# A hybrid block on one core: a new order of the stage between samples, and six of 32 scan inputs made by GpSimd

## The chip, the cores and the metric

One core of a Trainium2 chip runs the whole program. The metric is the device time of one execution in microseconds (us), the median of several runs. Engines: PE is TensorE, DVE is VectorE, ACT is ScalarE, POOL is GpSimd, SP is SyncE, which here only issues DMAs.

## The reference, cut to what matters

For each of 8 samples (800 tokens of 128 channels) three layers follow one another:

```
x = x + mamba(groupnorm(x))        # state space layer; its output gets the residual groupnorm(x) too
t = t + attention(layernorm(t))    # 8 heads of 16, softmax, projection, relu
t = t + experts(layernorm(t))      # two experts per sample, after all samples
```

The inner part of the mamba layer, with 256 inner channels and 16 states:

```
xz = xr @ W_in.T;  xc, z = split(xz)
xc = silu(causal_conv4(xc) + conv_b)
dt_in, Bm, Cm = split(xc @ W_xproj.T)
dt = softplus(dt_in @ W_dt.T + b_dt)
dA = exp(dt * A);  dBu = (dt * xc) * Bm        # u = dt * xc, times B
h = dA_t * h + dBu_t;  y = sum_states(h * C_t) # the scan over 32 time steps
out = ((y + xc * D) * silu(z)) @ W_out.T;  out = out * rsqrt(mean(out^2)) * ln_w
```

## The kernel before, in words

Every engine has its own list of instructions, written out by hand in one Python function per engine, and semaphores (`sig`) tie them together. All work is float32 except the bfloat16 parts of the attention scores.

Time is cut in turns. `turns` (line 481 on) calls `steps(n, m, f)` and then `front(n, m, f)` for each turn, where m is the sample whose scan runs, n = m - 1 the sample in attention, and f = m + 1 the sample that is prepared. Turn 0 has no n, turn 7 no f, and turn 8 only n.

**Steps.** The scan of one sample is 32 steps (`NSTEP`). A step i covers 32 channels times 4 states on 128 partitions and 800 columns. On each engine it is:
- DVE: the product of u and b, `PS<-u_rep,b_rep` (L1237, called P(i) below), into PSUM bank 2, then the scan `hst<-dA,PS` (L1242, S(i)), which reads dA from SBUF and the product from PSUM.
- ACT: `dA<-dt_rep,a_sb` (L924, the decay), up to three steps ahead, since dA has three buffers.
- POOL: `...<-hst,c_rep` (L794, G(i)), the multiplication by C. It waits for S(i) and also for P(i+1), in the code `pool.wait_ge(dbu_ready.sem, dbu_ready.at(m, i + 2))`.
- PE: once per four steps, `sum_states` (L1389).

hst has two buffers, so S(i) waits for G(i-2):

```
if i >= 2:
    dve.wait_ge(g_ready.sem, g_ready.at(m, i - 1))
```

**Attention among the steps.** In steps `MAX_FROM` = 5 to `MAX_TO` = 7 the row maxima of the scores are found: 50 items, each of PE products (L1508, L1509, L1514), a ReLU on ACT (L965) and a DVE reduction (L1263). The items need `k_neg`, made by DVE (L1258) from `k_stack`, which comes by DMA. From `UNIT_FROM` = 9 to `UNIT_TO` = 30 come 100 units: PE scores (L1542), ACT exponential (L975), PE product with V (L1527), and per 25 units one DVE copy to o_raw (L1284).

**Front.** Between S(31) and the next sample's S(0), each engine finishes attention of n and the mamba output of m, and prepares f. The chains of DVE in the order of the code: divide the attention (L1135, L1140); convolve chunk 0 (L1101, L1104); sum_up and gate of m (L1080, L1151); convolve chunk 1; attention residual t2 and the sums of its norm, norm2 (L1158, L1020 to L1030); the RMS factor of m (`rms_v` L1164, then POOL's reciprocal root L727, then L1168); relu of dt (L1173); residual of m (L1177); softplus rest, dt and u of f (L1117 to L1128); the sums of norm1 (L1020 to L1030); `x_sum` of f (L1187); statistics of the next sample's group norm (L1044 to L1063). ACT in the front: silu of both chunks (L850), squares of m's output (L873), xd (L877), |dt| (L858), exp and ln (L898, L902), silu of z (L854), then norm1 applied (L840) and the decay of the next step 0 (L924). norm1 is applied with POOL's result of L727 and L737, which wait for the sums on DVE (`ln1_var`).

Of the kernel before, what the change touches and what calls it, by code (L numbers as in the profile page):

```python
# [32 lines left out]
def mamba_attention_moe(nc, x, w_in_t, conv_w, conv_b, w_xp_t, w_dt_t, b_dt, a_log, d_skip, w_out_t,  # L33
# [46 lines left out]
    with ctx:  # L80
# [239 lines left out]
        dbu_ready = sig("dbu_ready", NSTEP)  # L320
# [23 lines left out]
        parts_out = sig("parts_out", 32)  # L344
# [479 lines left out]
        def _(act):  # L824
# [19 lines left out]
            def front(n, m, f):  # L844
# [30 lines left out]
                if f is not None:  # L875
                    act.wait_ge(xd_up.sem, xd_up.at(f, 1))
                    nc.scalar.copy(xd[:, :], wide(2)).then_inc(xd_ready.sem, 1)  # L877
                    absolute(0)
                    exp_of(f, 0)
                    ln_of(f, 0)  # L880
# [4 lines left out]
                    nc.scalar.activation(dt_sb[:, 1, :], wide(0), ACT.Relu, bias=b_dt_sb[:, 1:2]).then_inc(dt_relu1.sem, 1)  # L885
                if m is None and f is not None:
# [796 lines left out]
```

## Time and profile before

| | before |
|---|---|
| median of 3 runs | 1777.21 us (1776.51 to 1780.95) |
| the profiled execution | 1784.96 us, span of its instructions 1783.4 us |
| DVE busy | 1381.3 us, 77% |
| PE busy | 1210.5 us, 68% |
| ACT busy | 1089.9 us, 61% |
| POOL busy | 702.1 us, 39% |
| mean granted TensorE clock | 0.823 |

How to read it: the time is that of the engine or chain that ends last in each stage, and the stages repeat with the turns. A busy share below 100% on every engine means that the bound moves between engines, or that one waits for another; which of them must be read stage by stage from the timeline of a turn.

### The profile page before, as it was taken

Reading aid. Unit: us, or ns where it says so; the run is one execution under the profiler, and the core shown is the slowest. Engines: PE = TensorE matmul, PEld = TensorE weight load, DVE = VectorE, ACT = ScalarE, POOL = GpSimd, SP = SyncE. Lnnn points to the kernel's source line nnn. Section 1 sums busy time; section 2 is a strip of 40 time slices with the busy share of each in tenths; the row PEclk is TensorE's granted clock in tenths of the full one; section 3 lists DMA queues with packets and bytes.
Section 4 is the critical chain, followed back from the end, with each engine's and each line's share of the span. In section 5 each row is a group of like instructions: output and inputs, shape, how many; then the busy total and the mean of one; then the engine's idle time right before and its main releaser. Section 6 shows DMA issues by size and latency. Waiting matters only on the chain. (4 is left out here: it accounts for less than half of the span.)

```text
span 1783.4 us, 21758 instructions
## 1 busy us (share of the span) xinstructions
PE 1210.5 (68%) x7072; PEld 520.4 (29%) x7072; DVE 1381.3 (77%) x2336; ACT 1089.9 (61%) x1993; POOL 702.1 (39%) x399
## 2 busy tenths in 40 slices
PE   5124577867786678667876787578847864884991
PEld 2002231242224222422233223222323222222871
DVE  4798788988898889888988988798879973401575
ACT  3432767676767677667757776677677844663430
POOL 3364235524561356225622553256324640000354
PEclk8555688978898789878996899689968996895996
DMA  2441634145414641363228231814072405003541
GB/s 68 158 138 28 187 56 158 38 168 102 149 47 141 129 146 41 122 158 123 64 69 210 74 113 42 228 57 138 23 193 84 139 10 111 2 1 94 164 128 51
DMA packets 94021, 185.08 MB, mean 104 GB/s; under 512 B 15512, under 2 KB 48564, under 8 KB 93908
## 3 DMA queue, kind: packets, MB, share of 16 engines
q1 hardware_dynamic: 92500, 180.41, 35.0%
q0 software_dynamic: 1408, 3.29, 0.6%
q8 instruction: 55, 0.90, 0.2%
q14 instruction: 58, 0.48, 0.1%
HBM read 146.47 MB, written 36.86 MB: 103 GB/s over the span
## 5 line engine op out<-in xcount | busy, mean ns | idle before, releaser
L1242 DVE TENSOR_TENSOR_SCAN hst<-dA,PS 128x800 f32<-128x800 f32 x256 | 466.2, 1821 | 36.8 <-ACT dA L924 3.6
L975 ACT ACTIVATE probs<-PS 128x400 f32<-128x400 f32 x800 | 343.6, 526 | 119.5 <-PE PS L1542 119.4
L1542 PE MATMUL PS<-q_stack,k_stack 99*128 99x400 bf16 (+1 forms) x896 | 238.4, 358 | 88.7 <-ACT probs L975 41.7
L924 ACT ACTIVATE dA<-dt_rep,a_sb 128x775 f32<-128x775 f32 x256 | 245.6, 962 | 74.4 <-DVE hst L1242 62.9
L1237 DVE TENSOR_TENSOR PS<-u_rep,b_rep 128x800 f32<-128x800 f32 x256 | 267.5, 1045 | 19.0 <-DMA u_rep<-u_dram 6.5
L965 ACT ACTIVATE probs<-PS 128x400 f32<-128x400 f32 x400 | 201.7, 504 | 120.1 <-PE PS L1509 97.5
L1263 DVE CUSTOM_DVE_ANT_0 probs<-PS,probs 128x400 f32<-128x400 f32 x400 | 219.7, 573 | 42.6 <-PE PS L1514 17.2
L1527 PE MATMUL PS<-probs,v_ext 128*32 128x400 f32 (+1 forms) x1792 | 206.1, 538 | 30.7 <-DVE o_raw L1284 24.1
L1508 PE MATMUL PS<-k_stack,q_stack 96*128 96x400 bf16 (+1 forms) x448 | 142.4, 354 | 96.7 <-DVE k_neg L1258 96.7
L794 POOL TENSOR_TENSOR dt_sb<-hst,c_rep 128x800 f32<-128x800 f32 x72 | 135.8, 1886 | 153.5 <-DVE PS L1237 153.5
L727 POOL TENSOR_TENSOR norm_r<-norm_r,neg_half 100x8 f32<-100x8 f32 x24 | 40.8, 1702 | 390.6 <-DVE norm_r L1030 371.9
L794 POOL TENSOR_TENSOR sp_l<-hst,c_rep 128x800 f32<-128x800 f32 x72 | 135.5, 1882 | 117.3 <-DVE PS L1237 117.0
L1542 PEld LDWEIGHTS PS<-q_stack,k_stack 99*128 99x128 bf16 (+1 forms) x896 | 66.8, 98 | 337.9 <-ACT probs L975 229.4
L1514 PE MATMUL PS<-k_stack,q_stack 96*128 96x400 bf16 (+1 forms) x448 | 142.0, 353 | 9.7 <-DVE q_max L1263 9.1
L1389 PE MATMUL PS<-dt_sb,fold 128*32 128x512 f32 (+1 forms) x288 | 109.6, 625 | 50.9 <-POOL lnT L794 36.6
L1509 PE MATMUL PS<-k_neg,q_stack 96*128 96x400 bf16 (+1 forms) x448 | 141.8, 352 | 0.0
L794 POOL TENSOR_TENSOR conv_acc<-hst,c_rep 128x800 f32<-128x800 f32 x32 | 60.1, 1878 | 182.6 <-DVE PS L1237 182.6
L1389 PE MATMUL PS<-sp_l,fold 128*32 128x512 f32 (+1 forms) x288 | 109.6, 626 | 0.0
L794 POOL TENSOR_TENSOR xd<-hst,c_rep 128x800 f32<-128x800 f32 x40 | 75.2, 1881 | 64.7 <-DVE PS L1237 64.7
L794 POOL TENSOR_TENSOR lnT<-hst,c_rep 128x800 f32<-128x800 f32 x40 | 76.1, 1902 | 37.3 <-DVE PS L1237 34.0
L1389 PE MATMUL PS<-xd,fold 128*32 128x512 f32 (+1 forms) x160 | 67.6, 549 | 19.7 <-POOL sp_l L794 10.6
L1284 DVE COPY o_raw<-PS 128x400 f32<-128x400 f32 x32 | 18.2, 567 | 77.9 <-PE PS L1527 77.9
(223 smaller groups left out, 2093.8 us busy)
## 6 DMA issues: line engine op xcount, KB each, us to landing
b_rep<-b_dram SPq DMA_DIRECT2D x64, 400.0 KB, 3.5
c_rep<-c_dram SPq DMA_DIRECT2D x64, 400.0 KB, 3.8
dt_rep<-dt_dram SPq DMA_DIRECT2D x64, 400.0 KB, 6.3
u_rep<-u_dram SPq DMA_DIRECT2D x64, 400.0 KB, 6.3
q_stack<-parts_dram SPq DMA_DIRECT2D x96, 100.0 KB, 4.7
k_stack<-parts_dram SPq DMA_DIRECT2D x96, 100.0 KB, 6.2
dt_dram<-dt_sb SPq DMA_DIRECT2D x16, 400.0 KB, 3.5
u_dram<-sp_l SPq DMA_DIRECT2D x16, 400.0 KB, 3.8
```

What stands on the lines that cost most here:

```text
L794: nc.gpsimd.tensor_tensor(g(i), hst[:, i % 2, :], c_rep[:, rnd % NBB, :], ALU.mult).then_inc(g_ready.sem, 1)
L924: nc.scalar.activation(dA[:, i % NDA, :].rearrange("p (j t) -> p j t", t=T)[:, :, 1:T], dt_rep[:, gi, :].rearrange("p (j t) -> p j t", t=T ...
L965: nc.scalar.activation(probs[:, k % NPROB, :], bank(5 + 2 * (k % 2), HALF), ACT.Relu).then_inc(relu_ready.sem, 1)
L975: nc.scalar.activation(probs[:, j % NPROB, :], bank(4 + j % 3, HALF), ACT.Exp, scale=ATT_SCALE).then_inc(probs_ready.sem, 1)
L1237: nc.vector.tensor_tensor(dbu, u_rep[:, gi, :], b_rep[:, k, :], ALU.mult).then_inc(dbu_ready.sem, 1)
L1242: nc.vector.tensor_tensor_scan(hst[:, i % 2, :], dA[:, i % NDA, :], dbu, 0.0, ALU.mult, ALU.add).then_inc(scan_done.sem, 1)
L1263: nc.vector.tensor_tensor_reduce(probs[:, j % NPROB, :], bank(4 + 2 * (j % 2), HALF), probs[:, j % NPROB, :], 1.0, LOWEST, ALU.add, ALU.ma ...
L1389: last = nc.tensor.matmul(PS[gi * DG:(gi + 1) * DG, at:at + width], fold[:, :], g(rnd * NG + gi)[:, at:at + width], start=(sg == 0), stop= ...
L1508: nc.tensor.matmul(bank(5 + 2 * (k % 2), HALF)[strip], q, k_stack[0:KST, h, HALF:TOK], start=True, stop=False)
L1514: last = nc.tensor.matmul(bank(4 + 2 * (j % 2), HALF)[strip], q, k_stack[0:KST, h, 0:HALF], start=True, stop=True)
L1527: last = nc.tensor.matmul(PS[32 * q:32 * (q + 1), 7 * BANK:7 * BANK + HALF], v_ext[keys, kt, h, :], probs[keys, j % NPROB, :], start=(kt = ...
L1542: last = nc.tensor.matmul(bank(4 + j % 3, HALF)[strip], k_stack[:, h, kt * P:kt * P + strip.stop - strip.start], q_stack[:, h, q0:q0 + HAL ...
```

## The change: what it does

1. **Products by POOL.** In steps 10, 14, 18, 22, 26 and 30 (`POOL_STEPS`) DVE makes no product. POOL makes it (`product`, L791 in the new code) right behind G(i-3), into `sp_e[:, 0, :]` in SBUF, and the scan of such a step reads both operands from SBUF. Semaphores count both kinds of product apart (`by_vector`, `by_pool`).
2. **Row maxima later.** `MAX_FROM, MAX_TO` go from 5, 7 to 7, 9, so the 100 units start at step 11 instead of 9 and still end before step 30. The first `k_neg` is made ahead of step 7's product, and the stacks of q load when q's own parts have been stored.
3. **Front.** On DVE both convolutions stand in a row; relu, softplus rest, dt and u of f go ahead of the RMS work of m; `x_sum` leaves DVE (PE adds x with a second product into PSUM, ACT copies it out after `ln1_var`); `group_var` goes behind S(0) and `group_apply` behind S(1). On ACT xd, |dt|, exp and ln go ahead of the squares. On PE the chunk products move and out_project is cut in halves.

The diff, cut to its core:

```diff
+        dbu_pool = sp_e[:, 0, :]
...
-        MAX_FROM, MAX_TO = 5, 7
+        MAX_FROM, MAX_TO = 7, 9
+        POOL_STEPS = [i for i in range(MAX_TO, NSTEP) if i % NG == 2]
...
             def load_u(m, ck, gi):
                 if ck > 0:
-                    sp.wait_ge(dbu_ready.sem, dbu_ready.at(m, ck * NSG * NG - NG + gi + 1))
+                    sp.wait_ge(dbu_ready.sem, dbu_ready.at(m, by_vector(ck * NSG * NG - NG + gi + 1)))
+                    sp.wait_ge(dbu_pool_ready.sem, dbu_pool_ready.at(m, by_pool(ck * NSG * NG - NG + gi + 1)))
...
+            def product(m, i):
+                ck, sg, gi, rnd = step(i)
+                pool.wait_ge(u_in[gi].sem, u_in[gi].at(m, 16 * (ck + 1)))
+                pool.wait_ge(b_in[rnd % NBB].sem, b_in[rnd % NBB].at(m, 16 * (rnd // NBB + 1)))
+                nc.gpsimd.tensor_tensor(dbu_pool, u_rep[:, gi, :], b_rep[:, rnd % NBB, :], ALU.mult).then_inc(dbu_pool_ready.sem, 1)
...
                         if i + 1 < NSTEP:
-                            pool.wait_ge(dbu_ready.sem, dbu_ready.at(m, i + 2))
+                            pool.wait_ge(dbu_ready.sem, dbu_ready.at(m, by_vector(i + 2)))
                         nc.gpsimd.tensor_tensor(g(i), hst[:, i % 2, :], c_rep[:, rnd % NBB, :],
                                                 ALU.mult).then_inc(g_ready.sem, 1)
                         if n is not None and i == MAX_FROM:
                             softplus_of_second_chunk(m)
+                        if i + 3 in POOL_STEPS:
+                            product(m, i + 3)
...
                 if f is not None:
                     silu_x(1)
+                    act.wait_ge(xd_up.sem, xd_up.at(f, 1))
+                    nc.scalar.copy(xd[:, :], wide(2)).then_inc(xd_ready.sem, 1)
+                    absolute(0)
+                    exp_of(f, 0)
+                    ln_of(f, 0)
                 if m is not None:
                     act.wait_ge(out_up.sem, out_up.at(m, 1))
                     for k in range(NT):
                         last = nc.scalar.activation(sq[:, k, :], tokens(4)[:, k, :], ACT.Square, accum_out=rms_v[:, 0, k:k + 1])
                     last.then_inc(rms_sq.sem, 1)
                 if f is not None:
-                    act.wait_ge(xd_up.sem, xd_up.at(f, 1))
-                    nc.scalar.copy(xd[:, :], wide(2)).then_inc(xd_ready.sem, 1)
-                    absolute(0)
-                    exp_of(f, 0)
-                    ln_of(f, 0)
                     silu_z(0)
                     silu_z(1)
...
+                    act.wait_ge(gn_tok_up.sem, gn_tok_up.at(f, 1))
+                    if m is not None:
+                        act.wait_ge(ln1_var.sem, ln1_var.at(m, 1))
+                    nc.scalar.copy(x_sum[:, :, :], tokens(6)).then_inc(xs_ready.sem, 1)
...
                     convolve(0)
+                    convolve(1)
...
+                if f is not None:
+                    dve.wait_ge(dt_abs.sem, dt_abs.at(f, 1))
+                    nc.vector.tensor_scalar(dt_sb[:, 0, :], wide(2), b_dt_sb[:, 0:1], 0.0, ALU.add, ALU.max).then_inc(dt_relu0.sem, 1)
+                    low_part(0, fthen)
+                    dt_and_u(0)
                 if m is not None:
                     dve.wait_ge(rms_sq.sem, rms_sq.at(m, 1))
...
-                    nc.vector.tensor_tensor(x_sum[:, :, :], x_tok[:, :, :], tokens(6), ALU.add).then_inc(xs_ready.sem, 1)
...
                 for i in range(NSTEP):
+                    if n is not None and i == MAX_FROM:
+                        negate_keys(0)
...
-                        nc.vector.tensor_tensor(dbu, u_rep[:, gi, :], b_rep[:, k, :], ALU.mult).then_inc(dbu_ready.sem, 1)
+                        source = dbu_pool if i in POOL_STEPS else dbu
+                        if i not in POOL_STEPS:
+                            nc.vector.tensor_tensor(dbu, u_rep[:, gi, :], b_rep[:, k, :], ALU.mult).then_inc(dbu_ready.sem, 1)
...
-                        nc.vector.tensor_tensor_scan(hst[:, i % 2, :], dA[:, i % NDA, :], dbu, 0.0,
+                        nc.vector.tensor_tensor_scan(hst[:, i % 2, :], dA[:, i % NDA, :], source, 0.0,
                                                      ALU.mult, ALU.add).then_inc(scan_done.sem, 1)
...
                     if f is not None and i == 0:
+                        group_var(f)
+                    if f is not None and i == 1:
                         group_apply(f)
```

Two places where instructions move. The first is POOL's list in a turn's steps, around steps 11 to 18 (`...<-hst,c_rep` is G of one step, by the buffer it writes; `sp_e<-u_rep,b_rep` is the new product). Before, from G(10) on:

```order
L794 TENSOR_TENSOR conv_acc<-hst,c_rep 128x800 x2
L794 TENSOR_TENSOR dt_sb<-hst,c_rep 128x800
L794 TENSOR_TENSOR sp_l<-hst,c_rep 128x800
L794 TENSOR_TENSOR xd<-hst,c_rep 128x800
L794 TENSOR_TENSOR lnT<-hst,c_rep 128x800
```

In the changed kernel, from G(10) on:

```order
L813 TENSOR_TENSOR conv_acc<-hst,c_rep 128x800 x2
L791 TENSOR_TENSOR sp_e<-u_rep,b_rep 128x800
L813 TENSOR_TENSOR dt_sb<-hst,c_rep 128x800
L813 TENSOR_TENSOR sp_l<-hst,c_rep 128x800
L813 TENSOR_TENSOR xd<-hst,c_rep 128x800
L813 TENSOR_TENSOR lnT<-hst,c_rep 128x800
L791 TENSOR_TENSOR sp_e<-u_rep,b_rep 128x800
```

A product stands between G(11) and G(12), and the next one behind G(15), so POOL has five operations per four steps where it had four.

The second is DVE's list in the front, behind the last small operation of norm2. Before:

```order
L1030 TENSOR_TENSOR norm_r<-norm_mv 100x8
L1164 TENSOR_SCALAR rms_v<-rms_v 100x8
L1168 SCALAR_TENSOR_TENSOR hst<-PS,rms_v,ln_w_sb 100x128 x8
L1173 TENSOR_SCALAR dt_sb<-PS,b_dt_sb 128x800
L1177 TENSOR_TENSOR t<-x_sum,hst 100x1024
L1117 TENSOR_SCALAR lnT<-sp_e 128x800
L1118 TENSOR_TENSOR lnT<-sp_e,lnT 128x800
L1121 TENSOR_TENSOR dt_sb<-dt_sb,lnT 128x800
L1126 TENSOR_TENSOR dt_sb<-dt_sb,sp_l 128x800
L1128 TENSOR_TENSOR sp_l<-dt_sb,xc 128x800
L1020 BN_STATS norm_stats<-t 100x6 x8
```

In the changed kernel:

```order
L1055 TENSOR_TENSOR norm_r<-norm_mv 100x8
L1187 TENSOR_SCALAR dt_sb<-PS,b_dt_sb 128x800
L1142 TENSOR_SCALAR lnT<-sp_e 128x800
L1143 TENSOR_TENSOR lnT<-sp_e,lnT 128x800
L1146 TENSOR_TENSOR dt_sb<-dt_sb,lnT 128x800
L1151 TENSOR_TENSOR dt_sb<-dt_sb,sp_l 128x800
L1153 TENSOR_TENSOR sp_l<-dt_sb,xc 128x800
L1193 TENSOR_SCALAR rms_v<-rms_v 100x8
L1197 SCALAR_TENSOR_TENSOR hst<-PS,rms_v,ln_w_sb 100x128 x8
L1203 TENSOR_TENSOR t<-x_sum,hst 100x1024
L1045 BN_STATS norm_stats<-t 100x6 x8
```

The work of sample f (relu, softplus rest, dt, u) now stands ahead of the RMS work of m, and the sums of norm1 come straight behind that.

## Rows read from the trace of the kernel before

**Rows 1.** Windows of turn 2: length, busy PE, PEld, DVE, ACT, POOL, clock, DMA
```profile
409.34:450.64 41.30, 33.51 (x191) 14.06 (x191) 33.26 (x112) 27.30 (x53) 12.36 (x7) 0.91 0.38 81
450.64:529.49 78.85, 63.59 (x434) 16.23 (x435) 71.79 (x54) 60.78 (x124) 48.02 (x25) 0.89 0.31 106
529.49:570.62 41.13, 28.56 (x144) 17.81 (x142) 33.79 (x77) 25.61 (x43) 10.35 (x8) 0.87 0.30 102
```

**Rows 2.** Timeline, steps 28 and 29 of turn 2: start, length, engine, line, operation, [idle before]
```profile
520.17 1.82 DVE L1242 TENSOR_TENSOR_SCAN hst<-dA,PS 128x800 f32<-128x800 f32 x1
...
522.02 1.00 DVE L1237 TENSOR_TENSOR PS<-u_rep,b_rep 128x800 f32<-128x800 f32 x1
...
523.15 1.82 DVE L1242 TENSOR_TENSOR_SCAN hst<-dA,PS 128x800 f32<-128x800 f32 x1
...
520.21 1.92 POOL L794 TENSOR_TENSOR lnT<-hst,c_rep 128x800 f32<-128x800 f32 x1 [1.18 <-DVE PS L1237]
```

**Rows 3.** Timeline, steps 21 to 23 of turn 2, and L1242 over the whole run
```profile
498.43 1.00 DVE L1237 TENSOR_TENSOR PS<-u_rep,b_rep 128x800 f32<-128x800 f32 x1
498.44 2.74 POOL L800 TENSOR_TENSOR conv_acc<-xc,z_act 128x800 f32<-128x800 f32 x1
...
501.14 1.92 POOL L794 TENSOR_TENSOR lnT<-hst,c_rep 128x800 f32<-128x800 f32 x1
501.42 2.49 DVE L1237 TENSOR_TENSOR PS<-u_rep,b_rep 128x800 f32<-128x800 f32 x1
...
L1242 DVE TENSOR_TENSOR_SCAN hst<-dA,PS x256: 1819/1821/1823, 63.3 to 1448.4; 128x800 f32<-128x800 f32 x128
```

**Rows 4.** Timeline, DVE, start of the maxima in turn 2
```profile
411.37 0.57 DVE L1258 TENSOR_SCALAR k_neg<-k_stack 96x1600 bf16<-96x1600 bf16 x1 [2.03 <-DMA k_stack<-parts_dram]
...
414.09 0.57 DVE L1263 CUSTOM_DVE_ANT_0 probs<-PS,probs 128x400 f32<-128x400 f32 x1 [2.15 <-PE PS L1514]
```

**Rows 5.** Timeline, turn 2: first and last exponentials of the units; first o_raw copy
```profile
455.81 1.69 ACT L975 ACTIVATE probs<-PS 128x400 f32<-128x400 f32 x4 [2.37 <-PE PS L1542]
...
524.00 2.07 ACT L975 ACTIVATE probs<-PS 128x400 f32<-128x400 f32 x5
...
475.56 0.57 DVE L1284 COPY o_raw<-PS 128x400 f32<-128x400 f32 x1 [2.04 <-PE PS L1527]
```

**Rows 6.** Timeline, DVE, second half of the front of turn 2
```profile
548.01 0.17 DVE L1164 TENSOR_SCALAR rms_v<-rms_v 100x8 f32<-100x8 f32 x1
...
551.68 2.16 DVE L1168 SCALAR_TENSOR_TENSOR hst<-PS,rms_v,ln_w_sb 100x128 f32<-100x128 f32 x8 [3.50 <-POOL rms_v L727]
...
554.71 1.22 DVE L1177 TENSOR_TENSOR t<-x_sum,hst 100x1024 f32<-100x1024 f32 x1
...
559.65 0.99 DVE L1128 TENSOR_TENSOR sp_l<-dt_sb,xc 128x800 f32<-128x800 f32 x1
...
562.96 0.17 DVE L1030 TENSOR_TENSOR norm_r<-norm_mv 100x8 f32<-100x8 f32 x1
563.04 1.22 DVE L1187 TENSOR_TENSOR x_sum<-x_tok,PS 100x1024 f32<-100x1024 f32 x1
...
570.62 1.82 DVE L1242 TENSOR_TENSOR_SCAN hst<-dA,PS 128x800 f32<-128x800 f32 x1 [0.55 <-ACT dA L924]
```

**Rows 7.** Timeline, ACT and POOL in the same stretch
```profile
545.79 0.30 ACT L873 ACTIVATE hst<-PS 100x128 f32<-100x128 f32 x1
...
550.00 1.64 POOL L727 TENSOR_TENSOR rms_v<-rms_v,neg_half 100x8 f32<-100x8 f32 x1
550.97 0.93 ACT L858 ACTIVATE sp_e<-PS,b_dt_sb 128x800 f32<-128x800 f32 x1 [1.70 <-PE PS L1377]
...
555.39 0.87 ACT L902 ACTIVATE sp_l<-sp_e 128x800 f32<-128x800 f32 x1
...
565.15 3.18 ACT L840 ACTIVATE probs<-t,norm_r 100x128 f32<-100x128 f32 x8 [1.51 <-POOL norm_r L737]
...
569.65 0.94 ACT L924 ACTIVATE dA<-dt_rep,a_sb 128x775 f32<-128x775 f32 x1
```

More of the change, by code:

```diff
@@ L343, in mamba_attention_moe @@
         v_copied = sig("v_copied")
-        parts_out = sig("parts_out", 32)
+        parts_out = [sig(f"parts_out{i}", 16) for i in range(2)]
         NSTK = 2 * len(Q_PARTS)
@@ L432, in share, with by_vector, by_pool @@
             return range(min(lo * work // (end - first), work), min(hi * work // (end - first), work))
+        def by_vector(k):
+            return sum(i not in POOL_STEPS for i in range(k))
+        def by_pool(k):
+            return sum(i in POOL_STEPS for i in range(k))
         def max_share(i):
@@ L866, in front @@
                     act.wait_ge(proj_up.sem, proj_up.at(n, 1))
-                    nc.scalar.activation(oT[:, :], wide(6), ACT.Relu, bias=proj_b_sb[:, 0:1]).then_inc(att_ready.sem, 1)
+                    nc.scalar.activation(oT[:, :], wide(4), ACT.Relu, bias=proj_b_sb[:, 0:1]).then_inc(att_ready.sem, 1)
                 if f is not None:
                     silu_x(1)
+                    act.wait_ge(xd_up.sem, xd_up.at(f, 1))
[3 more added lines that the diff above has]
+                    ln_of(f, 0)
                 if m is not None:
@@ L1152, in front @@
                                             ALU.mult).then_inc(y_ready[1].sem, 1)
-                if f is not None:
-                    convolve(1)
                 if n is not None:
@@ L1203, in front @@
                     group_mean(f + 1)
-                    group_var(f + 1)
                 assert n is None or dve_order_p.count == dve_order_p.per_turn, dve_order_p.count
@@ L1222, in low_parts, with negate_keys @@
                     dve.wait_ge(qk_parts.sem, qk_parts.at(n, i + 1))
+                def negate_keys(half):
+                    dve.wait_ge(stacks_in[half].sem, stacks_in[half].at(n, 16 * NSTK))
+                    nc.vector.tensor_scalar(k_neg[:, 4 * half:4 * half + 4, :], k_stack[0:KST, 4 * half:4 * half + 4, 0:HALF],
+                                            -1.0, None, ALU.mult).then_inc(k_neg_ready.sem, 1)
                 for i in range(NSTEP):
+                    if n is not None and i == MAX_FROM:
+                        negate_keys(0)
                     if m is not None:
@@ L1454, in front @@
                     last.then_inc(attT_up.sem, 1)
+                if f is not None:
+                    pe.wait_ge(silu_done.sem, silu_done.at(f, 2))
+                    x_project(1).then_inc(xd_up.sem, 1)
                 if m is not None:
@@ L1458, in front @@
                         pe.wait_ge(y_ready[ck].sem, y_ready[ck].at(m, 1))
-                    out_project(range(NT)).then_inc(out_up.sem, 1)
+                    out_project(range(NT // 2))
                 if f is not None:
-                    for ck in range(NC_):
-                        pe.wait_ge(silu_done.sem, silu_done.at(f, ck + 1))
-                        last = x_project(ck)
-                    last.then_inc(xd_up.sem, 1)
                     pe.wait_ge(xd_ready.sem, xd_ready.at(f, 1))
                     over_spans(2, w_dt_sb[DT0:P, 0:P], xd[DT0:P, :]).then_inc(dt_up.sem, 1)
+                if m is not None:
+                    out_project(range(NT // 2, NT)).then_inc(out_up.sem, 1)
+                if f is not None:
+                    if m is not None:
+                        pe.wait_ge(y_summed.sem, y_summed.at(m, NC_))
                     project_in(0, 2).then_inc(xz_up.sem, 1)
@@ L1470, in front @@
                         pe.wait_ge(t2_ready.sem, t2_ready.at(n, 1))
+                    pe.wait_ge(x_in.sem, x_in.at(f, 16))
                     for k in range(NT):
-                        last = nc.tensor.transpose(PS[0:TT, 6 * BANK + k * C:6 * BANK + (k + 1) * C], xnT[:, k * TT:(k + 1) * TT], ident[:, :])
+                        o = PS[0:TT, 6 * BANK + k * C:6 * BANK + (k + 1) * C]
+                        nc.tensor.matmul(o, xnT[:, k * TT:(k + 1) * TT], ident[:, :], start=True, stop=False)
+                        last = nc.tensor.matmul(o, ident[0:TT, 0:TT], x_tok[:, k, :], start=False, stop=True)
                     last.then_inc(gn_tok_up.sem, 1)
```

53 lines of the change are left out of this document (25 added, 28 removed).

## The prediction, made before the changed kernel was run

> **What bounds the kernel now.** I read the stages of a turn first, then the timeline inside each, then who ended the waits. Turn 2 stands for turns 1 to 6. The stretch of the row maxima lasts 41.30 us, steps 7 to 31 last 78.85, from the start of S(31) to the next S(0) pass 41.13 [rows 1]. VectorE has the highest busy share in the last two, 71.79 of 78.85 and 33.79 of 41.13; in the maxima TensorE and VectorE share it.
>
> In a step VectorE alternates: a scan of 1.82 us, a product of 1.00, and gaps, together 2.98 from scan to scan (520.17 to 523.15); I use 3.0 [rows 2]. GpSimd starts G within 0.04 us of the next scan, takes 1.92, and is then idle until the next product is done (1.18 idle). So GpSimd looks as if it had over a third of its time free, and that is what the change spends. The next two things to see decide whether it has.
>
> First, the two engines exclude each other in some operations. At 501.14 GpSimd began a G (both operands in SBUF), and 0.28 us later VectorE began a product, again with both operands in SBUF. It took 2.49 instead of 1.00, and ended 0.85 us after G [rows 3]. The other way round, at 498.43 and 498.44, VectorE's product came first and took its 1.00, and GpSimd's operation took 2.74. A scan, which has only dA in SBUF and the product in PSUM, ran beside a G in nearly every step and never took more than 1823 ns [rows 3]. The Trainium skill states this as a rule (SBUF — State Buffer, Who interferes with whom): a VectorE instruction with two SBUF inputs and a GpSimd one that reads SBUF exclude each other for the whole instruction, the later one being blocked. By that rule a scan that reads its product from SBUF is exposed as well, which no row here shows.
>
> Second, hst has two buffers, so S(i) waits for G(i-2). Today G(i-2) ends at about the end of S(i-1), and the product hides the rest.
>
> **The change part by part.**
>
> *Products by GpSimd.* Count from the start of S(i-2), where i is a step whose product GpSimd makes. G(i-3) runs 0.04 to 1.92. P(i-1) runs 1.85 to 2.85, and the new product, issued behind G(i-3), finds VectorE ahead of it, as at 498.44: it ends at about 4.65 (1.92 + 2.74) [rows 3]. S(i-1) runs 3.0 to 4.8. G(i-2) is queued behind the new product: 4.65 to 6.55. S(i) waits for it, until 6.6, where VectorE alone would have been ready at 4.9. In that instant GpSimd has already begun G(i-1), whose waits are met. If the scan with two SBUF operands is excluded like the product at 501.42, it starts at 8.4 and ends at 10.2; P(i+1) and S(i+1) follow, S(i+1) starting at 11.4. Before, this distance was three steps, 9.0. The price is 2.3 us per such step (rounding 2.4 down for gaps that overlap). The bounds: if GpSimd's work costs nothing, the step is worth -1.1 (the 3.0 of a step less 1.82 and a gap); if scan and G go side by side, S(i) runs 6.6 to 8.4 and S(i+1) starts at 9.5, +0.5; if the new product gets ahead of P(i-1), +2.6. I take 2.3, since the nearest row for two SBUF operands against a G is the 2.49, in full.
>
> In step 10 the new product is made during the maxima and costs nothing, and only the exclusion of S(10) by G(9) is left: 1.8 of waiting less the 1.1 saved, 0.7. So turn 0, which has no attention, pays 6 x 2.3 = 13.8, and turns 1 to 7 each pay 5 x 2.3 + 0.7 = 12.2.
>
> *Maxima two steps later.* VectorE's work is the same, only in another order. What goes is the wait of k_neg for the stacks, 2.03, since steps 5 and 6 (6.0 us) now stand ahead, and the wait for the first score, 2.15, since k_neg is made a step before it is needed [rows 4]. -4.2 per turn. In the units the first o_raw copy waits 2.04 for TensorE [rows 5]; the price of step 14 lies ahead of that copy and takes its place: -2.0.
>
> *Do the units now become the bound?* They ran from 455.81 to 526.07, 70.3 us [rows 5], with two decays of 0.94 in it that now lie ahead: 68.4. With the same distances to the scans they need some 71 from S(11) to S(31). VectorE: 78.85 - 6.0 - 2.0 + 12.2 = 83 from S(9), 76 from S(11) [rows 1]. So they stay hidden while VectorE pays its price, and would be the floor if it did not.
>
> Per turn 1 to 7: 12.2 - 4.2 - 2.0 = +6.0, x 7 = +42.
>
> *The front.* Today VectorE finishes norm2's sums at 548.0, waits 3.50 for GpSimd, and does the RMS work while ACT makes exp and ln [rows 6, 7]. In the new order it waits at the same place for |dt|, 550.97 + 0.93 = 551.9; that time hardly moves, because silu of chunk 1 still waits for the gate of m, which now stands behind both convolutions, and the half of out_project that is gone from TensorE's queue ahead of chunk 1's projection is replaced by the other half ahead of dt. Relu ends at 552.9, the softplus rest starts with exp at about 554, and dt and u end at 558.7, 1.9 us earlier than the 560.6 of today. But u is not what S(0) waits for: it waits 0.55 for ACT's decay at 569.65, which stands behind norm1's application, 565.15 to 568.33 [rows 6, 7]. And that chain starts later: squares (2.2 us, 545.79 to 548.0) now follow ln, which ends 556.26, so they are done at 558.5; then rms_v 0.17 at 558.7, GpSimd's root 1.64 and hand-over to 560.7, 2.16 for L1168, 1.22 for the residual, 2.5 for the sums (560.64 to 563.13): 566.6 instead of 563.13. From there to S(0) it is 7.5 us as today; ACT's copy of x_sum lies beside GpSimd's root. S(0) starts at 574.1 instead of 570.62: +3.4. The 1.22 of x_sum that VectorE no longer does lay beside that chain and brings nothing. group_var, two small operations of 0.16 and 0.15, is now behind S(0): +0.35. Together 3.75, in 7 fronts: +26. Bounds for a front: -1.6 (x_sum and group_var off the path, no later chain) and +5, if TensorE at its lower clock makes more of it late.
>
> On SP's queue the q stacks go out earlier and the loads of u wait for GpSimd's products too, which are done steps ahead: 0.
>
> **The sum.** 42 + 13.8 + 26 = +82 us on the profiled execution's 1784.96, 1867. The median of the runs is 7.7 lower, so 1859.
>
> **The rivals.**
>
> *A: scan and G do not exclude each other.* A scan is not the product of the row, and only the exclusion of products is seen. Then the price is 0.5, VectorE would need 67 from S(11), and the 71 of the units are the floor: 6.0 - 5 - 0.7 = about 0 per turn. Turn 0 +3, the fronts +26: 1777 + 29 = 1806. Against it: the row at 501.42 is about operands, not the operation, and the cited rule names two SBUF inputs without an exception.
>
> *B: faster.* GpSimd's product fits into its idle time and the front's chain isn't later. It decides if S(i) finds G(i-2) done within 0.1 us of S(i-1)'s end, and if norm1's sums end before 563. Then turn 0 gains 6 x 1.1 = 6.6; turns 1 to 7 gain the 4.2, but the units' floor lets only about 1 of the rest through, 1.2 each; the fronts give back 1.2 each: 6.6 + 8.4 + 8.4 = -23, 1754. For it: GpSimd is idle over a third of each step. Against: 1.92 + 1.92 + 1.92 in two steps of 3.0 do not fit, whatever the exclusion does.
>
> *C: a heavier price.* Exclusion delays G so that sum_states and the copies wait as well, 3.5 a step: 1.2 x 41 = 49 more, 1908.
>
> *D: forecast price, but the front free:* 1833, within my own range.
>
> **How the numbers follow.** The forecast with D has 0.68, A 0.15, B 0.11, C 0.06. Time 1859; its own range is 1825 to 1885 (front between -1.6 and +5, price between 1.7 and 2.6). The range of 8 in 10 takes in A: 1800 to 1885. A measurement tells 0.3%, some 5 us. Slower by more: forecast, C and all but 0.01 of A, 0.88. Faster: all but 0.01 of B, 0.10. The same: 0.02.
>
> **What would show it.** S(i-2) to S(i+1) 11.4 around a step with GpSimd's product, against 9.0; the new scan (L1270, from sp_e) recorded at about 3.6 us or starting 3.5 late, with a G right beside it; GpSimd's product near 2.7; k_neg without a wait; S(31) to S(0) at 44.5 against 41.13, with ln1_var's sums ending 3.5 later. The forecast is wrong if that scan takes 1.82 beside a G (A), if S(i) follows S(i-1) by 1.9 (B), or if S(31) to S(0) is 41 or less.

## The result, and the profile after

| | before | after |
|---|---|---|
| median of 4 runs each (lowest to highest), us | 1779.08 (1776.51 to 1781.71) | 1869.51 (1864.83 to 1872.68) |
| profiled execution, us | 1784.96 | 1869.83 |
| its span, us; mean granted clock | 1783.4; 0.823 | 1868.2; 0.808 |

The changed kernel is slower: the ratio of the times is 1.0506, with a 95% interval of 1.0477 to 1.0535. The forecast was 1859 us. The profiled execution of the kernel before lies 5.9 us above its median and that of the changed kernel at its median, so the medians differ by 90.4 us and the profiles by 84.9.

The first view is the windows of turn 2, laid as those of before [rows 1]: the maxima (now end of S(7) to S(9)), the steps from S(9) to S(31), and the front. The columns are those of rows 1.

```profile
442.63:481.34 38.71, 33.29 (x172) 14.22 (x174) 32.79 (x111) 25.56 (x51) 14.18 (x8) 0.85 0.23 71
481.34:562.06 80.72, 65.54 (x437) 17.49 (x430) 70.75 (x43) 59.34 (x122) 57.15 (x28) 0.88 0.29 98
562.06:607.50 45.44, 31.50 (x165) 21.38 (x163) 32.41 (x75) 26.58 (x44) 9.11 (x7) 0.84 0.40 137
```

The steps stretch now holds 22 steps and not 24, and is still 1.9 us longer than before. VectorE is busy for 1.0 us less in it, GpSimd for 9.1 us more. The starts of the scans give the account of the whole span. From S(0) to S(31), turn 0 went from 96.55 to 109.80 us, +13.3. Turn 2 went from 143.20 to 148.97, +5.8, and turns 1 to 7 together took 41.8 more. From S(31) to the next S(0), turn 0 went from 42.91 to 47.91 and turn 2 from 41.14 to 45.42, in all seven +31.7. The first S(0) starts 2.5 us earlier. The sum is 84.3, and the span is 84.8 longer.

The second view is of the scans: the costliest groups of the changed kernel (busy us, mean ns of one, idle time before them), and under them what the view of the source line gives for the same two forms (shortest, median, longest ns).

```profile
L1270 DVE TENSOR_TENSOR_SCAN hst<-dA,PS 128x800 f32<-128x800 f32 x208 | 378.8, 1821 | 54.1 <-ACT dA L949 26.6
L1270 DVE TENSOR_TENSOR_SCAN hst<-dA,sp_e 128x800 f32<-128x800 f32 x48 | 160.0, 3334 | 56.6 <-POOL dt_sb L813 38.7
L791 POOL TENSOR_TENSOR sp_e<-u_rep,b_rep 128x800 f32<-128x800 f32 x48 | 116.8, 2434 | 0.0
...
L1270 DVE TENSOR_TENSOR_SCAN hst<-dA,PS x208: 1819/1821/1822, 60.8 to 1532.7; 128x800 f32<-128x800 f32 x104
L1270 DVE TENSOR_TENSOR_SCAN hst<-dA,sp_e x48: 2973/3331/3442, 92.5 to 1527.8; 128x800 f32<-128x800 f32 x48
```

A scan that reads its product from PSUM still takes at most 1822 ns, though a G runs beside it in nearly every step. All 48 that read it from sp_e in SBUF take 2973 ns or more. The 1821 to 3331 is 1.5 us each, 72 us in all, and before them stands another 56.6 us of idle time, mostly for a G.

The third view is the timeline of steps 14 and 15, then of the product for step 18, in turn 2.

```profile
495.72 1.87 POOL L813 TENSOR_TENSOR dt_sb<-hst,c_rep 128x800 f32<-128x800 f32 x1
497.56 1.88 POOL L813 TENSOR_TENSOR sp_l<-hst,c_rep 128x800 f32<-128x800 f32 x1
497.79 3.33 DVE L1270 TENSOR_TENSOR_SCAN hst<-dA,sp_e 128x800 f32<-128x800 f32 x1 [1.84 <-POOL dt_sb L813]
501.15 1.00 DVE L1262 TENSOR_TENSOR PS<-u_rep,b_rep 128x800 f32<-128x800 f32 x1
502.29 1.82 DVE L1270 TENSOR_TENSOR_SCAN hst<-dA,PS 128x800 f32<-128x800 f32 x1
...
507.27 1.88 POOL L791 TENSOR_TENSOR sp_e<-u_rep,b_rep 128x800 f32<-128x800 f32 x1
507.58 2.44 DVE L1262 TENSOR_TENSOR PS<-u_rep,b_rep 128x800 f32<-128x800 f32 x1
```

S(14) waits 1.84 us for the G of S(12), which stood in GpSimd's queue behind a new product. The moment it may start, GpSimd has begun the next G. That G ends at 499.44, and the scan ends 1.68 us later, at 501.12, nearly a whole scan's length: it did its work after the G, not beside it. From S(12), at 491.14, to S(15) it is 11.15 us. The 9.0 of the prediction is what these three steps take where nothing else waits: 8.96 in turn 0 before, and 8.96 in turn 2 of the changed kernel without GpSimd's products (the first experiment). In turn 2 of the kernel before they took 11.45, because the first o_raw copy and its wait [rows 5] stood among them; so there the price does not show in this distance. Last, the new product for step 18, at 507.27, came just before VectorE's next one, which took 2.44 instead of 1.00.

The fourth view is the start of the maxima on VectorE and two items of their second half. The three windows under them are the start of the second half in the changed kernel (S(8) starts at 459.85), then in the kernel before (S(6) starts at 431.90). Their columns are those of rows 1.

```profile
439.20 0.57 DVE L1242 TENSOR_SCALAR k_neg<-k_stack 96x1600 bf16<-96x1600 bf16 x1
...
442.55 0.55 DVE L1290 CUSTOM_DVE_ANT_0 probs<-PS,probs 128x400 f32<-128x400 f32 x1
...
464.89 0.57 DVE L1290 CUSTOM_DVE_ANT_0 probs<-PS,probs 128x400 f32<-128x400 f32 x1 [0.42 <-issue]
...
465.89 0.57 DVE L1290 CUSTOM_DVE_ANT_0 probs<-PS,probs 128x400 f32<-128x400 f32 x1 [0.42 <-issue]
...
460.00:463.00 3.00, 0.87 (x4) 0.44 (x4) 2.75 (x6) 0.50 (x1) 3.00 (x2) 0.87 0.00 0
463.00:466.00 3.00, 3.00 (x11) 1.37 (x9) 1.75 (x7) 1.51 (x3) 2.92 (x2) 0.50 0.00 0
...
432.05:435.05 3.00, 1.72 (x10) 0.64 (x9) 2.92 (x6) 1.45 (x4) 3.00 (x2) 1.00 0.00 0
```

Both waits of before, 2.03 and 2.15 [rows 4], are gone. The first half of the maxima, scan to scan, fell from 24.38 to 19.03. The second half rose from 18.74 to 21.50. TensorE was busy for 0.87 of three microseconds there (460 to 463), beside VectorE's scan. From 463 its granted clock was 0.50, that is 1.2 GHz, and the maxima came one per 1.00 us with 0.42 idle before each. Before, TensorE was busy for 1.72 of the same three microseconds, and its clock stayed at 1.00.

The fifth view is the timeline of the front of turn 2: what ended the longer waits.

```profile
564.77 0.59 DVE L1160 RECIPROCAL o_rec<-PS 100x16 f32<-100x16 f32 x4 [0.88 <-PE PS L1632]
...
585.28 1.05 DVE L1187 TENSOR_SCALAR dt_sb<-PS,b_dt_sb 128x800 f32<-128x800 f32 x1 [3.91 <-ACT sp_e L879]
...
593.97 2.16 DVE L1197 SCALAR_TENSOR_TENSOR hst<-PS,rms_v,ln_w_sb 100x128 f32<-100x128 f32 x8 [1.75 <-POOL rms_v L739]
...
600.07 1.64 POOL L739 TENSOR_TENSOR norm_r<-norm_r,neg_half 100x8 f32<-100x8 f32 x1 [6.14 <-DVE norm_r L1055]
602.03 3.18 ACT L861 ACTIVATE probs<-t,norm_r 100x128 f32<-100x128 f32 x8 [0.93 <-POOL norm_r L749]
...
607.50 1.82 DVE L1270 TENSOR_TENSOR_SCAN hst<-dA,PS 128x800 f32<-128x800 f32 x1 [3.32 <-ACT dA L949]
```

The front begins with a wait of 0.88 us for TensorE, which hands over the attention (L1632); before, VectorE began that division 1.76 us after the start of S(31), without a wait:

```profile
531.25 0.59 DVE L1135 RECIPROCAL o_rec<-PS 100x16 f32<-100x16 f32 x4
```

Then VectorE waits 3.91 us for |dt| where it waited 3.50 for the RMS root [rows 6]. Then it waits 1.75 for that root as well. norm1's root starts 38.0 us after S(31); before it was 33.7 (VectorE's last step ahead of it, at 562.96, is in [rows 6], and the root began at 563.20). S(0) now waits 3.32 for the decay. From norm1's root to S(0) it is 7.4 us, as before.

### The profile page after: what moved, and what is told of

It reads as the page before. It is cut to its first block and busy times, and to the rows that moved or that the text cites. A ratio compares the mean times of both kernels' runs of the same rounds, so it can differ in the third digit from the quotient of the medians.

```text
span 1868.2 us, 22307 instructions
## 1 busy us (share of the span) xinstructions
PE 1270.3 (68%) x7264; PEld 566.7 (30%) x7264; DVE 1410.7 (76%) x2280; ACT 1096.3 (59%) x2001; POOL 820.9 (44%) x447
## 3 DMA queue, kind: packets, MB, share of 16 engines
q1 hardware_dynamic: 92500, 180.41, 34.3%
## 5 line engine op out<-in xcount | busy, mean ns | idle before, releaser
L1270 DVE TENSOR_TENSOR_SCAN hst<-dA,PS 128x800 f32<-128x800 f32 x208 | 378.8, 1821 | 54.1 <-ACT dA L949 26.6
L1262 DVE TENSOR_TENSOR PS<-u_rep,b_rep 128x800 f32<-128x800 f32 x208 | 233.5, 1123 | 12.0 <-DMA u_rep<-u_dram 2.6
L1565 PE MATMUL PS<-probs,v_ext 128*32 128x400 f32 (+1 forms) x1792 | 213.7, 556 | 32.0 <-DVE o_raw L1311 25.8
L1270 DVE TENSOR_TENSOR_SCAN hst<-dA,sp_e 128x800 f32<-128x800 f32 x48 | 160.0, 3334 | 56.6 <-POOL dt_sb L813 38.7
L1546 PE MATMUL PS<-k_stack,q_stack 96*128 96x400 bf16 (+1 forms) x448 | 152.1, 376 | 44.2 <-DVE k_neg L1242 41.6
L1552 PE MATMUL PS<-k_stack,q_stack 96*128 96x400 bf16 (+1 forms) x448 | 151.0, 374 | 15.7 <-DVE q_max L1290 15.1
L1547 PE MATMUL PS<-k_neg,q_stack 96*128 96x400 bf16 (+1 forms) x448 | 150.3, 370 | 0.0
L791 POOL TENSOR_TENSOR sp_e<-u_rep,b_rep 128x800 f32<-128x800 f32 x48 | 116.8, 2434 | 0.0
L1416 PE MATMUL PS<-sp_l,fold 128*32 128x512 f32 (+1 forms) x288 | 115.2, 627 | 0.0
L813 POOL TENSOR_TENSOR lnT<-hst,c_rep 128x800 f32<-128x800 f32 x40 | 88.4, 2210 | 28.8 <-DVE PS L1262 28.6
L1416 PE MATMUL PS<-xd,fold 128*32 128x512 f32 (+1 forms) x160 | 80.3, 635 | 24.0 <-POOL sp_l L813 12.8
```

Of the source, the lines that this page charges most:

```text
L1262: nc.vector.tensor_tensor(dbu, u_rep[:, gi, :], b_rep[:, k, :], ALU.mult).then_inc(dbu_ready.sem, 1)
L1270: nc.vector.tensor_tensor_scan(hst[:, i % 2, :], dA[:, i % NDA, :], source, 0.0, ALU.mult, ALU.add).then_inc(scan_done.sem, 1)
L1416: last = nc.tensor.matmul(PS[gi * DG:(gi + 1) * DG, at:at + width], fold[:, :], g(rnd * NG + gi)[:, at:at + width], start=(sg == 0), stop= ...
L1546: nc.tensor.matmul(bank(5 + 2 * (k % 2), HALF)[strip], q, k_stack[0:KST, h, HALF:TOK], start=True, stop=False)
L1552: last = nc.tensor.matmul(bank(4 + 2 * (j % 2), HALF)[strip], q, k_stack[0:KST, h, 0:HALF], start=True, stop=True)
L1565: last = nc.tensor.matmul(PS[32 * q:32 * (q + 1), 7 * BANK:7 * BANK + HALF], v_ext[keys, kt, h, :], probs[keys, j % NPROB, :], start=(kt = ...
```

## The experiments

My theory: the GpSimd products cost most of it, because the scan that reads SBUF and GpSimd's operations shut each other out; the front costs the rest, through norm1's later sums; the maxima pay a little. Four kernels took the change apart first.

The ratios are to runs of the kernel before that were made along with these kernels: their median is 1779.75 us for the first four (no products, products alone, the place of the product, the maxima later) and 1781.81 us for the others.

**No products on GpSimd.** The changed kernel, with

```diff
-POOL_STEPS = [i for i in range(MAX_TO, NSTEP) if i % NG == 2]
+POOL_STEPS = []
...
```

> The changed kernel with all products of u and b on VectorE again, so only the new front and the later maxima are left of the change. My theory (each step with a GpSimd product costs 1.5 to 2.3 us net, and the steps' floor comes back to what it was before): S(11) to S(31) falls from 74.0 to about 67 us per turn, the stretch S(31) to the next S(0) stays at about 45, and the kernel takes about 1815 us (1805 to 1825), some 50 below the changed kernel and 38 above the kernel before. Rival 1 (GpSimd's products are harmless and the front and the maxima cost it all): about 1865. Rival 2 (the maxima pay in full and only the fronts cost): about 1791.

Measured: 1792.82 us (1791.81 to 1795.96), ratio to before 1.0081, interval 1.0057 to 1.0105. So the products cost the changed kernel 77 us, and front and maxima together 13. This is rival 2's number, not mine. S(11) to S(31) fell to 65.8 us, below even the 67 that I expected, with the front at 44.5. The 1815 missed by 22 us. Two terms of the expectation make that up: S(11) to S(31) fell by 8.2 us in a turn and not by 7 (8 us in seven turns), and the some 50 us that it took off are seven times those 7, with nothing for turn 0, which gave 13.2.

**Products alone.** The kernel before with only the six products on GpSimd, in the steps of the change (10, 14, 18, 22, 26 and 30):

```diff
+dbu_pool = sp_e[:, 0, :]
+POOL_STEPS = [i for i in range(MAX_TO, NSTEP) if i % NG == 2]
...
-nc.vector.tensor_tensor(dbu, u_rep[:, gi, :], b_rep[:, k, :], ALU.mult)
+source = dbu_pool if i in POOL_STEPS else dbu
+if i not in POOL_STEPS:
+    nc.vector.tensor_tensor(dbu, u_rep[:, gi, :], b_rep[:, k, :], ALU.mult)
...
+if i + 3 in POOL_STEPS:
+    product(m, i + 3)
```

With the maxima at steps 5 and 6 the same line gives the same six steps, since 10 is the first one that fits from 7 on.

> The kernel before with the six products on GpSimd and nothing else of the change. My theory: every scan that reads the product from SBUF takes about 3.3 us instead of 1.8, S(11) to S(31) rises by 7 to 9 us in turns 1 to 7 and by 13 in turn 0, and the time is about 1860 us (1845 to 1875). Rival A (the scan and GpSimd's work only lose half a microsecond per step): about 1801. Rival B (VectorE is relieved of six products of a microsecond): below 1777.

Measured: 1868.37 us (1864.69 to 1869.48), ratio 1.0495, interval 1.0469 to 1.0520. That is +89, 1.85 us per step with a GpSimd product, and within what my theory gave. Rivals A and B are out. From S(5) to S(31) turn 0 took 13.3 us more, 2.2 per such step; no attention work runs there, so it is not the attention's TensorE work, nor its clock, that pays this. The costliest groups of this kernel:

```profile
L1268 DVE TENSOR_TENSOR_SCAN hst<-dA,PS 128x800 f32<-128x800 f32 x208 | 378.7, 1821 | 30.6 <-ACT dA L945 2.8
L1268 DVE TENSOR_TENSOR_SCAN hst<-dA,sp_e 128x800 f32<-128x800 f32 x48 | 159.7, 3328 | 62.4 <-POOL dt_sb L813 43.9
L791 POOL TENSOR_TENSOR sp_e<-u_rep,b_rep 128x800 f32<-128x800 f32 x48 | 117.9, 2456 | 0.0
```

**Only the place of the product.** The kernel before, every product still on VectorE, those of the same six steps written to SBUF:

```diff
-nc.vector.tensor_tensor(dbu, u_rep[:, gi, :], b_rep[:, k, :], ALU.mult)
+source = dbu_pool if i in POOL_STEPS else dbu
+nc.vector.tensor_tensor(source, u_rep[:, gi, :], b_rep[:, k, :], ALU.mult)
```

> The kernel before, with VectorE still making every product, but those of the same six steps written to SBUF in place of PSUM; no work moves to another engine. If it is the scan's second SBUF operand that makes it and GpSimd's G shut each other out, these 48 scans rise from 1.82 to 3.3 us or their G from 1.92 to 3.4 and each such step costs 1.0 to 1.8 us: about 1835 us (1825 to 1860). If the price comes from GpSimd's extra product alone (its queue being longer), the scans stay at 1.82 and the time at 1777 (plus or minus 5).

Measured: 1830.99 us (1826.23 to 1832.62), ratio 1.0281, interval 1.0255 to 1.0307. No work changed its engine, and the kernel lost 51 us, 1.07 per such step. VectorE's products took 0.99 us into SBUF as against 1.00 into PSUM, so it is not the writing. So the scan's second SBUF operand alone is over half of the 89. The timeline of turn 0, where no attention work runs, shows who pays:

```profile
120.56 1.82 DVE L1245 TENSOR_TENSOR_SCAN hst<-dA,sp_e 128x800 f32<-128x800 f32 x1
120.60 3.46 POOL L796 TENSOR_TENSOR sp_l<-hst,c_rep 128x800 f32<-128x800 f32 x1 [1.17 <-DVE sp_e L1240]
...
123.24 1.67 DVE L1240 TENSOR_TENSOR PS<-u_rep,b_rep 128x800 f32<-128x800 f32 x1
```

Here the scan comes first by 0.04 us and keeps its 1.82; the G takes 3.46, and the next product then has to wait for the G and takes 1.67. So it went for 40 of the 48 scans; in the other 8, one in each turn, the scan took 3.3. In the changed kernel the G had come first and the scan took 3.33. Whichever starts second does its work after the other. The Trainium skill says this of a VectorE instruction with two SBUF inputs and a GpSimd one that reads SBUF (SBUF — State Buffer, Who interferes with whom). The traces agree for the scan in both orders: 3.33 us for the one and 3.46 for the other, in place of 1.82 and 1.88.

**A third buffer for the scans' states.** Two explanations of a step's price were left: the sum of what the two engines cannot do at once, or the scan's wait for a G two steps back, which the new product in GpSimd's queue makes late. A third buffer, from step 12 on, loosens that wait. It uses the second chunk of sp_e, and from step 14 on scan i waits for G(i-3):

```diff
+def state(i):
+    return hst[:, i % 2, :] if i < 12 else (hst[:, 0, :], hst[:, 1, :], sp_e[:, 1, :])[(i - 12) % 3]
...
-    dve.wait_ge(g_ready.sem, g_ready.at(m, i - 1))
+    dve.wait_ge(g_ready.sem, g_ready.at(m, i - 1 if i < 14 else i - 2))
```

> The kernel before with the six GpSimd products, and from step 12 on a third buffer for the scans' states, so that a scan waits for the G of three steps before and not of two. My theory (what two engines do with two SBUF operands each adds up, whatever the order: per four steps 3 products of 1.0, a scan of 1.8 and 5 GpSimd operations of 1.88 make 14.2 us): S(11) to S(31) stays at 71 to 75 us and the kernel at 1845 to 1868 us. Rival (the price is the wait of a scan for a late G, that is the order of GpSimd's queue): the period falls to VectorE's own 11 to 12 us per four steps, S(11) to S(31) to about 62 to 66 us, and the kernel to 1780 or less.

Measured: 1843.33 us (1842.45 to 1850.96), ratio 1.0345, interval 1.0319 to 1.0371. That is just under the 1845 that I had as the least. Its control is the kernel before with the third buffer alone:

> The kernel before with only the third state buffer from step 12 on, the control of the run above. Both theories: VectorE's own product and scan fill the 3.0 us of a step nearly, so little changes, 1765 to 1782 us; whatever it gains must be taken off what the run above gains.

Measured: 1780.67 us (1773.76 to 1787.25), ratio 0.9993, interval 0.9975 to 1.0011. The control is unchanged, so all 25 us that the third buffer gives belong to the products, and over 60 of their 89 stay. In turn 0 S(11) to S(31), five groups of four steps, took 62.55 us before, 73.65 with the products, and 71.00 with the third buffer too. Some of these groups also hold work that comes once per turn, VectorE's sum_up and GpSimd's gate product: before, S(15) to S(23) took 26.5 us and not 24.0. The first group, S(11) to S(15), is free of it: it took 12.02 us before, 14.16 with the products, 13.81 with the third buffer too. Three products of VectorE (1.00), one scan (1.82) and five GpSimd operations (1.88) add up to 14.2. With two buffers the kernel runs at this sum, with three 0.4 under it. The sum is thus an estimate, good to some tenths, and not a bound: the blocked one of a pair ends a little sooner than its own length after the other, as at S(14) of the changed kernel, 1.68 us after the G and not 1.82. The 11 to 12 us of the rival are not reached. From step 14 on no scan that reads the new product waits for a G any more; only S(10), ahead of the third buffer, still does, by 1.8 us. In the timeline of turn 0 such a scan starts 0.09 us after the end of the scan before it, and the exclusion is what is left:

```profile
120.83 1.87 POOL L818 TENSOR_TENSOR dt_sb<-hst,c_rep 128x800 f32<-128x800 f32 x1 [1.03 <-DVE PS L1265]
122.70 1.82 DVE L1273 TENSOR_TENSOR_SCAN hst<-dA,sp_e 128x800 f32<-128x800 f32 x1
122.74 3.45 POOL L818 TENSOR_TENSOR sp_l<-sp_e,c_rep 128x800 f32<-128x800 f32 x1
...
125.38 1.67 DVE L1265 TENSOR_TENSOR PS<-u_rep,b_rep 128x800 f32<-128x800 f32 x1
```

For the kernel before the same sum is 4 x 1.00 + 4 x 1.88 = 11.5, under VectorE's own 12.0 (four steps of 3.0), and GpSimd's idle third looked free. With the product in SBUF but made by VectorE it is 13.3, and S(11) to S(15) of turn 0 took 13.50.

**The maxima later, alone.** The kernel before with the maxima in steps 7 and 8, the first negation ahead of step 7, and the parts' stores awaited one by one:

```diff
-MAX_FROM, MAX_TO = 5, 7
+MAX_FROM, MAX_TO = 7, 9
...
+if n is not None and i == MAX_FROM:
+    negate_keys(0)
```

> The kernel before with only the maxima moved from steps 5 and 6 to steps 7 and 8, with the first negation ahead of step 7. My theory, from the trace of the changed kernel: the two waits of 2.03 and 2.15 us go, but half comes back in the second half of the maxima, and S(11) to S(31), where GpSimd then has all its steps still to do, does not get shorter: 0 to 2 us less per turn, 1762 to 1777 us. Rival (the waits only hid GpSimd's backlog, which now is not worked off): the same to 2 us more per turn, 1777 to 1793.

Measured: 1758.64 us (1755.92 to 1765.38), ratio 0.9887, interval 0.9865 to 0.9909. This part of the change is a gain of 21 us, 3.0 per turn with maxima, a little more than I allowed. It beats both kernels. S(5) to S(31) fell by 21.4 us in the seven turns: S(5) to S(9) gave 15.4 (in turn 2 from 49.17 to 46.49), S(11) to S(31) the other 6.1 (turn 3: 67.02 to 65.83; in turns 2 and 7 it rose by 0.4 and 0.3). So there was no backlog of GpSimd to be worked off.

**The new front, alone.** The change with POOL_STEPS empty, the maxima back at steps 5 and 6, and the stores of the parts awaited together again:

```diff
-MAX_FROM, MAX_TO = 7, 9
+MAX_FROM, MAX_TO = 5, 7
...
-POOL_STEPS = [i for i in range(MAX_TO, NSTEP) if i % NG == 2]
+POOL_STEPS = []
...
```

> The kernel before with only the new front (no GpSimd product, maxima where they were). From the kernel with the later maxima alone (1759) and the one with both (1793) the front would cost 34 us if the parts add: 1805 to 1817 us, the stretch from S(31) to the next S(0) at 44.5 us or more in place of 41.1. Rival (the front is free or a gain by itself, and costs only beside the later maxima, whose last copy comes later): 1770 to 1785 us.

Measured: 1819.45 us (1817.47 to 1820.52), ratio 1.0209, interval 1.0183 to 1.0235: +38, a little over the 1817 that I allowed, and rival D is out. With the later maxima the new front costs 34 (1792.82 less 1758.64). Alone it was 46.0 us from S(31) to S(0), beside them 44.5, because the wait for |dt| is longer (first line: new front alone; second: with the later maxima):

```profile
558.57 1.05 DVE L1190 TENSOR_SCALAR dt_sb<-PS,b_dt_sb 128x800 f32<-128x800 f32 x1 [5.39 <-ACT sp_e L882]
```

```profile
551.53 1.05 DVE L1188 TENSOR_SCALAR dt_sb<-PS,b_dt_sb 128x800 f32<-128x800 f32 x1 [3.90 <-ACT sp_e L880]
```

What makes |dt| later there is TensorE's clock. The product that |dt| hangs on, the projection of chunk 1 (L1457), took 3.03 us in the new front alone, at a granted clock of 0.50 (1.2 GHz), and 1.61 beside the later maxima, at 1.00. In both kernels TensorE had been idle for 2.44 us just before it (same order; under each line is its window, with the columns of rows 1):

```profile
551.18 3.03 PE L1457 MATMUL PS<-xc,w_xp_sb 128*128 128x512 f32 x4 [2.44 <-ACT xc L874]
...
551.18:554.21 3.03, 3.03 (x5) 1.66 (x6) 1.89 (x13) 0.00 (x0) 0.95 (x1) 0.50 0.02 5
```

```profile
545.64 1.61 PE L1457 MATMUL PS<-xc,w_xp_sb 128*128 128x512 f32 x4 [2.44 <-ACT xc L872]
...
545.64:547.25 1.61, 1.61 (x6) 1.00 (x7) 1.54 (x11) 0.00 (x0) 0.00 (x0) 1.00 0.06 10
```

The new front alone had it mostly or wholly at the lower clock in all seven fronts. Beside the later maxima it ran wholly at the lower clock only in turns 0 and 6, and in the kernel before at 1.00 in all. What makes TensorE fall to the lower clock in the one and not in the other stays open.

**RMS work first again.** The change without the GpSimd products, and with the RMS work ahead of dt on all three engines; both convolutions still in a row:

```diff
 ScalarE
-xd copy, |dt|, exp, ln of chunk 0
 squares
+xd copy, |dt|, exp, ln of chunk 0
 VectorE
-relu, softplus rest, dt, u of chunk 0
 rms_v, RMS scale
+relu
 t1
+softplus rest, dt, u of chunk 0
 TensorE
-x_project(1)
-out_project(range(NT // 2))
+out_project(range(NT))
+x_project(1)
...
-out_project(range(NT // 2, NT))
```

> The changed kernel without GpSimd products and with the sums for the RMS norm and the output projection ahead of dt again; both convolutions still stand in a row and the maxima are later. My theory (the new front's price is norm1's sums, which come 3.5 us later behind the RMS work that waits on GpSimd and ScalarE): S(31) to S(0) falls from 44.5 back to 41 to 42 us, the kernel to 1759 to 1768 us. Rival (the convolutions in a row or the new path of x_sum cost it): the stretch stays at 44 to 45 us and the kernel at 1788 to 1795.

Measured: 1768.21 us (1763.26 to 1777.66), ratio 0.9937, interval 0.9912 to 0.9962, at the upper end of what I allowed. The stretch fell from 44.5 to 41.7, and 25 of the front's 34 us came back. The timeline of its turn 2 shows the wait that had the place of this one:

```profile
545.03 0.17 DVE L1189 TENSOR_SCALAR rms_v<-rms_v 100x8 f32<-100x8 f32 x1 [2.45 <-ACT hst L895]
...
546.96 2.16 DVE L1193 SCALAR_TENSOR_TENSOR hst<-PS,rms_v,ln_w_sb 100x128 f32<-100x128 f32 x8 [1.75 <-POOL rms_v L740]
549.03 1.05 DVE L1198 TENSOR_SCALAR dt_sb<-PS,b_dt_sb 128x800 f32<-128x800 f32 x1
...
558.49 1.64 POOL L740 TENSOR_TENSOR norm_r<-norm_r,neg_half 100x8 f32<-100x8 f32 x1 [11.57 <-DVE norm_r L1056]
```

Relu no longer waits: |dt| is ready by the time the RMS scale is done. norm1's root starts 34.3 us after S(31) (at 524.21), and not 38.0. Some 10 us over the kernel with later maxima alone remain; in the two traces 5.7 of them lie between S(31) and S(0), 2.6 of that in turn 0. They go with what is left of the new front, the convolutions in a row, TensorE's x_sum and the group norm's work behind S(0); I did not take these apart. This kernel is faster than before, but not than the one with the later maxima alone.

## Why the prediction was right

The sum came out near the forecast: +84.8 us of span for +82, and 1869.5 for 1859 by the medians. Its main terms are right in mechanism. That it came so near is partly luck, since several terms were off and made up for each other.

- *The exclusion of scan and G* was right, and decided it. The scan from SBUF takes 3.33 us; turn 0 paid 13.3 us, forecast 13.8, and S(12) to S(15) took 11.15, forecast 11.4, against 8.96 without the products. The new product took 2.70 in the median, forecast 2.7. Rival A fell with it: the products alone gave 1868 and not 1801. So did B, by the same run. C wanted 3.5 a step, and turn 0 shows 2.2. The wait for a late G was part of the price that I worked out, and the third buffer, which takes it away, gave back 25 of the 89 us.
- *The price in turns 1 to 7* was too high. I had 12.2 less 2.0 for the wait ahead of the o_raw copy, 10.2 per turn. Between the changed kernel and the one without products S(0) to S(31) differs by 62.2 us in the seven turns, 8.9 each. The price of the steps was near: in turn 0 S(11) to S(31) paid 11.1 for five of them, forecast 11.5, and step 10 cost 0.75 in turn 2, forecast 0.7. Too small was what the price takes the place of. Attention made S(11) to S(31) 3.3 us longer in turn 2 than in turn 0 without the products, and 0.4 longer with them; so 2.9 us of its waits went, and I had 2.0.
- *The maxima* were too high as well: 4.2 per turn forecast, 3.0 measured alone and 2.9 beside the new front (from S(0) to S(31)). The waits of [rows 4] went as I said. What I did not have was the second half at TensorE's lower clock, which gave back 2.8 us in turn 2. The two errors, 1.3 and 1.3, cancel: +6.0 per turn was forecast, and 41.8 / 7 = 6.0 was measured. This is luck.
- *The floor of the units* was wrong. I said that they would need 71 us from S(11) to S(31) and so hold back the gain if VectorE didn't pay. Without products the stretch took 65.8. The 70 us that the units had taken before were not the least that they need. The row for the later maxima alone shows it, where they are dealt out to 20 steps and not 22, from 449.0 to 512.4 in place of 455.8 to 525.5. That the steps set their pace is my reading of this; no run shows how fast they could go.

```profile
L975 ACT ACTIVATE probs<-PS x100: 497/518/636, 449.0 to 512.4; 128x400 f32<-128x400 f32 x100
```

  This term did not enter the sum, only rivals A and B; that is why the sum held.
- *The front*: mechanism right, size low. I had 3.75 per front and 26 in all; it was 31.7. The start of norm1's root moved from 33.7 to 38.0 us after S(31), 4.3 and not 3.5, and turn 0's front paid 5.0, turn 6's 5.7. The 3.4 for the later chain is what turn 2 shows without GpSimd's products (44.52 less 41.14). The other 0.9 is the wait for TensorE at the front's start, 0.7 to 0.9 us in turns 1 to 5: it is there with the products alone too, in all seven turns, is gone with the third buffer, and is in no kernel without the products, so it belongs to the products and not to the new front. It was no term of my sum. In turn 0 the projection of chunk 1 ran at a granted clock of 0.50 and took 3.00 us, not 1.61, which I had only as a bound. Putting the RMS work first brought 25 of the front's 34 us back, so the later sums are the cause of most of it. S(0) did wait for the decay, 3.32. The first S(0), 2.5 us earlier, is no gain of the new front: it started at 59.8 in the kernel with later maxima alone, which has the old one, and at 63.9 in the one with the products alone.

## What to carry to other kernels

Before giving an idle GpSimd work, add up what it and VectorE cannot do at the same time: all of GpSimd's operations on SBUF and those of VectorE that read two SBUF operands. Here that sum was 11.5 of 12.0 us per four steps, so almost nothing was free though GpSimd was idle for a third; and moving an operation of 1.00 to an engine that needs 1.88 for it, with its result in SBUF, made the sum 14.2, and a plain group of four steps took 14.16. Where an operand lies is part of the price: PSUM for one operand of the scan was worth 1.07 us per such step with all the work in place. And a change of several parts is worth taking apart even when its sum is forecast well: one of the three was a gain of 1.1%.

## What the runs showed of the hardware that was not expected

- The exclusion is symmetric: the G behind a scan took 3.46 us (1.82 and 1.64 more), the scan behind a G 3.33. What is blocked counts as busy in the profile: with only the place of the product changed, VectorE's busy time rose from 1381.3 to 1438.4 us, from 77% to 79% of the span, with no more work in it.
- A gap of about 2 us in TensorE's work (busy 0.87 of 3.00) was followed by 6 us at a granted clock of 0.50, in a loop where VectorE waits for TensorE, and that cost most of the 2.8 us which the second half of the maxima lost. The gap was 2.13 us in all seven turns, and the clock fell after it in all seven; in turns 6 and 7 it stayed low for only some 3 us, and the second half took 20.1 and 20.0, not 21.5. In the kernel before the gap at this place was 1.28 us, and the clock stayed at 1.00 for the next 12 us in every turn. What sets how long the clock stays low, no run here settles.
- The same clock moved another stage: TensorE's projection of chunk 1 in the front took 3.03 us at 0.50 and 1.61 at 1.00, after the same 2.44 us of idle time, and that is the 1.5 us by which the new front alone is longer than beside the later maxima.
